# Scores ahead of the across-chunk products, and three reordered operations on VectorE, in a linear-attention and expert-routing kernel

## Chip, cores and metric

The kernel runs on one NeuronCore of one Trainium2 chip. The metric is device time in microseconds (us) of one execution. TensorE does the matrix products, VectorE (DVE in the profile) and ScalarE (ACT) read their results from PSUM, GpSimd (POOL) and SyncE (SP) do the rest and the transfers.

## The reference, cut to what matters

```python
def _linear_attention(x, Wq, Wk, Wv, Wo):
    Q = _phi((x @ Wq)...); K = _phi((x @ Wk)...); V = (x @ Wv)...
    S = jnp.cumsum(jnp.einsum('bhti,bhtj->bhtij', K, V), axis=2)
    z = jnp.cumsum(K, axis=2)
    num = jnp.einsum('bhti,bhtij->bhtj', Q, S)
    den = jnp.maximum(jnp.einsum('bhti,bhti->bht', Q, z), EPS_DEN)[..., None]
    return (num / den).transpose(0, 2, 1, 3).reshape(b, t, H * DV) @ Wo
x = x + _linear_attention(_layernorm(x, ln1_g, ln1_b), Wq, Wk, Wv, Wo)
h = _layernorm(x, ln2_g, ln2_b)
x = x + jax.nn.gelu(h @ Wf1, approximate=False) @ Wf2
```

x is 8 x 512 x 128, with 16 heads of 64; `_phi` is elu + 1. A layer norm follows, then a mixture of 8 experts (top 2 of a softmax gate, two layers of width 512), and a last layer norm.

## The kernel before

**Steps.** The attention part runs over 8 batch rows b and, in each, over 8 pairs of heads p: 64 steps, numbered g = 8b + p. The sequence of 512 is cut into four chunks of 128. Every engine has its own program, written out by hand in order, and the engines meet only through semaphores. Work of step g - 1 and g - 2 is mixed into step g, and in steps p = 2 to 7 the feed-forward part and the gate of batch row b - 1 are mixed in as well. After the 64 steps, 39 tiles of 256 routed rows go through the experts.

**TensorE in a step** issues, in this order: `columns(g-1)`, which is the state products K V of each chunk (L535, bank_u) and then the masked products inside the chunks (L542, banks_o); in p = 2 or 3 a transpose of another part; `across(g-1)`, the products of Q with the states of earlier chunks, which finish banks_o (L554); `scores(g)`, K Q inside the chunks (L563, banks_sc); `keys_t(g)`, transposes of K (L569, bank_u); the projections of Q and K for step g + 1 (L434 to L436, bank_q and bank_k); `wo_acc(g-2)` into bank_y; the projection of V (L458 to L460, into half of banks_sc); and `otr(g-1)`, the transposes of the normalised output (L446, into the other half of banks_sc).

**VectorE in a step**: `states(g-1)` sums the state products over chunks (L1296, L1298); `ot_low(g-2)` makes the low half of the transposed output from bank F, the second half of banks_sc, and from ScalarE's high half (oT_lo, L1129); then what the feed-forward part or the gate needs (`residual1`, `norm2` L1145, `norm3` L1145, `logits`, `place`); `normalise(g-1)` (L1282, L1284, L1286); `mask(g)` over both banks of scores (L1273); more of the other part (`residual2` L1191, `stats1`, `top2` L1218 to L1235, `g_high` L1187); and `q_phis`, `k_phis` of step g + 1 (L1257). In the last batch row the VectorE program also reads expert numbers into its registers (`expert(t)`, L1122) in steps p = 4 to 7, two behind each `mask`.

**ScalarE in a step**: `ktok_copy` (behind `keys_t`), the four exponential passes (L890 to L898), `v_copy`, and `ot_high(g-1)`, which makes oT_hi (L827) from the transposes. In p = 4 the four `gelus` (L856) come first; they read bank_q, bank_k and both halves of banks_sc.

Bank F is read by `ot_high` and `ot_low` and then overwritten by the scores, which is why `scores(g)` waits for `ot_lo` of g - 2. Bank E is read by `v_copy`. The state products share bank_u with the transposed keys.

Of the kernel before, what the change touches and what calls it, by code (L numbers as in the profile page):

```python
# [31 lines left out]
B, T, D = 8, 512, 128  # L32
CH = T // P
H, DH = 16, 64
PAIRS = H // 2
# [29 lines left out]
def build(nc, x_d, ln1_g, ln1_b, wq_d, wk_d, wv_d, wo_d, ln2_g, ln2_b, wf1_d, wf2_d,  # L65
# [5 lines left out]
    with ExitStack() as ctx:  # L71
# [154 lines left out]
        def ps(name, n):  # L226
# [23 lines left out]
        q_relu, q_exp, k_relu, k_exp, v_sb, kt_sb, ot_hi, yT_sb = (  # L250
            sem(n) for n in ("q_relu", "q_exp", "k_relu", "k_exp", "v_sb", "kt_sb", "ot_hi", "yT_sb"))
# [179 lines left out]
        def _(pe):  # L431
# [113 lines left out]
            def across(g):  # L545

                cur = g % 2
                pe.wait_ge(s_sb, g + 1)
                for c in range(1, CH):
                    if c == 2 and g + 1 < B * PAIRS:  # L550
                        pe.wait_ge(v_sb, min(CH + g + 1, 2 * CH * B))
                    for n, rows in enumerate(HEADS):
                        for h, hs in enumerate(HEADS):
                            mm = pe.matmul((bkG, bkH)[h][rows, blk(c, DV1)], qT[cur][hs, blk(2 * c + n, DH)],  # L554
                                           state[hs, c - 1, :], start=False, stop=(c == CH - 1))
                mm.then_inc(o_mm, 1)

            def scores(g):
                cur = g % 2
                for c in range(CH):  # L560
                    for n, rows in enumerate(HEADS):
                        for h, hs in enumerate(HEADS):
                            mm = pe.matmul((bkE, bkF)[h][rows, blk(c)], kT[cur][hs, blk(2 * c + n, DH)],  # L563
                                           qT[cur][hs, blk(c)], start=True, stop=True)
                mm.then_inc(sc_mm, 1)
# [12 lines left out]
            def step(b, p):  # L578
# [4 lines left out]
                if g > 0:  # L583
                    columns(g - 1)
                    if p == 2 and not first:
                        a_free(g - 1)
                        y_t(b - 1, bkA)
                    if p == 3 and not last:
                        b_free(g - 1)
                        front_t(b + 1)  # L590
                    across(g - 1)

                if g == 0:
                    pe.wait_ge(k_phi, 1)
                if g > 1:
                    pe.wait_ge(ot_lo, g - 1)
                if p == 4 and not first:
                    pe.wait_ge(gelu_sb, b * NF)
                scores(g)
                if p != 3:  # L600
                    keys_t(g)

# [515 lines left out]
        def _(dve):  # L1118
# [148 lines left out]
            def ot_low(g):  # L1267
                dve.wait_ge(ot_hi, g + 1)
                low(oT[1][:, :], bkF[:, :], oT[0][:, :]).then_inc(ot_lo, 1)
# [38 lines left out]
            def step(b, p):  # L1308
                g = b * PAIRS + p
                first, last = b == 0, b == B - 1  # L1310
                nxt = g + 1 < B * PAIRS
                if g > 0:
                    states(g - 1)
                if g > 1 and p != 4:
                    ot_low(g - 2)
                if not first:
                    if p == 0 and b > 1:
                        place(b - 2, bkA)
                    if p == 2:
                        residual1(b - 1, bkA)  # L1320
                    if p == 3:
                        norm2(b - 1)
                    if p == 4:
                        g_high(b - 1, (0, 1))
                    if p == 6:
                        norm3(b - 1)
                    if p == 7:
                        logits(b - 1, bkA)
                if g > 0:
                    normalise(g - 1)  # L1330
                mask(g)
                if last:
                    if p == 0:
                        plan_full_tiles()
# [539 lines left out]
```

## Time and profile before

| what | value |
|---|---|
| median of 3 runs | 725.69 us (724.81 to 725.83) |
| span of the profiled execution, first to last instruction | 696.0 us |
| its own total time | not given apart from the span; the median less the span is 29.69 us |
| TensorE matmul busy | 663.0 us, 95% |
| weight loads busy | 564.0 us, 81% |
| VectorE busy | 530.4 us, 76% |
| ScalarE busy | 426.3 us, 61% |
| GpSimd busy | 245.2 us, 35% |
| mean granted TensorE clock | 0.996 of full |

Busy times of engines overlap. The span is one execution under the profiler; the runs are timed without it. Times within the span are in us from its start.

### The profile page before, as it was taken

How to read it: one execution, taken by the hardware profiler on the slowest of the kernel's cores; microseconds unless marked ns; L12 is line 12 of the kernel's file. 1: busy time of each engine (PE TensorE's matmuls, PEld its weight loads, DVE VectorE, ACT ScalarE, POOL GpSimd, SP SyncE). 2: the span in 40 equal slices, each digit the busy share in tenths (PEclk: the TensorE clock that was granted, in tenths of full speed). 3: DMA queues.
4: the chain of work that ended last, by engine and by line, in shares of the span. 5: the costliest groups of instructions: out<-in, count | busy, mean ns of one | idle time of the engine just before them, and what ended most of it. 6: DMA issues, size and time to landing. Idle time of an engine off the chain costs nothing.

```text
span 696.0 us, 23152 instructions
## 1 busy us (share of the span) xinstructions
PE 663.0 (95%) x9314; PEld 564.0 (81%) x9314; DVE 530.4 (76%) x1565; ACT 426.3 (61%) x846; POOL 245.2 (35%) x271
## 2 busy tenths in 40 slices
PE   3899999999999999999999999999988999999995
PEld 2678888888888788888888887887778989999983
DVE  4867787887878788877878786898787777666674
ACT  4565576558466845765584668456644655666646
POOL 6200013025313512331253134123315557766664
PEclk9999999999999999999999999999999999999999
DMA  7330010001100100100011001001031224354536
GB/s 251 105 67 17 3 32 17 17 19 48 32 10 13 60 17 15 51 17 17 18 48 32 11 10 32 17 15 36 2 87 47 71 81 131 108 131 148 165 130 185
DMA packets 46521, 40.27 MB, mean 58 GB/s; under 512 B 9104, under 2 KB 41232, under 8 KB 46416
## 3 DMA queue, kind: packets, MB, share of 16 engines
q1 hardware_dynamic: 35360, 25.25, 13.1%
q0 software_dynamic: 4784, 10.39, 4.4%
q10 hardware_dynamic: 6272, 3.16, 1.5%
q8 instruction: 75, 1.23, 0.8%
q14 instruction: 30, 0.25, 0.1%
HBM read 23.12 MB, written 15.66 MB: 56 GB/s over the span
## 4 chain that ended last, share of the span: by engine, by line
PE 78%; DVE 12%; ACT 5%; issue 2%; DMA 1%; POOL 0%; DVEq 0%; ACTq 0%; POOLq 0%
PE banks_o L721 9%; PE banks_sc L563 8%; PE banks_o L542 6%; PE banks_o L554 4%; PE bank_u L535 4%; PE bank_u L569 4%; PE bank_q L434 3%; PE bank_q L436 3%; PE bank_q L435 3%; PE banks_sc L446 3%; PE bank_k L434 2%; PE bank_k L436 2%; PE bank_k L435 2%; DVE work L1257 2%; PE banks_sc L434 2%; PE bank_y L434 2%
## 5 line engine op out<-in xcount | busy, mean ns | idle before, releaser
L1723 POOL DMA_INDIRECT routed_rows<-routed,slot x64 | 63.2, 988 | 148.8 <-PE banks_sc L563 117.1
L827 ACT ACTIVATE work<-bank_u 128x384 f32<-128x384 f32 x64 | 31.5, 492 | 107.5 <-PE bank_u L569 107.5
L1273 DVE TENSOR_TENSOR work<-banks_sc,causal 128x1024 f32<-128x1024 f32 x64 | 77.9, 1218 | 0.6 <-PE banks_sc L563 0.6
L721 PE MATMUL banks_o<-w,work 128*128 x624 | 76.2, 275 | 0.0
L721 PEld LDWEIGHTS banks_o<-w,work 128*128 128x128 f32 x624 | 72.9, 192 | 0.3 <-issue 0.2
L563 PE MATMUL banks_sc<-work 64*64 64x128 f32 x2048 | 70.0, 274 | 1.1 <-ACT v_aug L827 0.7
L542 PE MATMUL banks_o<-v_aug,work 128*64 128x65 f32 x2048 | 70.6, 221 | 0.0
L1257 DVE SCALAR_TENSOR_TENSOR work<-bank_q,work 128x512 f32<-128x512 f32 x64 | 43.8, 684 | 29.4 <-ACT work L892 29.2
L1691 POOL TENSOR_SCALAR ve<-mv 128x4 f32<-128x4 f32 x24 | 4.7, 194 | 174.5 <-DVE mv L1139 174.3
L542 PEld LDWEIGHTS banks_o<-v_aug,work 128*64 128x64 f32 x2048 | 65.3, 138 | 0.0
L1257 DVE SCALAR_TENSOR_TENSOR work<-bank_k,work 128x512 f32<-128x512 f32 x64 | 44.2, 690 | 24.0 <-ACT work L898 24.0
L563 PEld LDWEIGHTS banks_sc<-work 64*64 64x64 f32 x2048 | 55.3, 133 | 8.1 <-DVE oT_lo L1129 2.7
L1713 POOL TENSOR_TENSOR gT_lo<-work,gT_hi 128x512 fp32r<-128x512 f32 x28 | 37.1, 1347 | 46.6 <-DVE gT_hi L1187 46.6
L1813 POOL DMA_INDIRECT expert_results<-work x40 | 40.1, 1004 | 21.5 <-ACT work L1023 11.3
L890 ACT ACTIVATE work<-bank_q 128x512 f32<-128x512 f32 x64 | 38.4, 600 | 14.5 <-PE bank_q L436 13.7
L1813 POOL DMA_INDIRECT expert_results<-work,xg_more x38 | 38.2, 1005 | 24.5 <-ACT work L1023 17.3
L1286 DVE TENSOR_TENSOR work<-banks_o,rden 128x512 f32<-128x512 f32 x64 | 44.3, 692 | 2.2
L1129 DVE TENSOR_TENSOR oT_lo<-banks_sc,oT_hi 128x512 fp32r<-128x512 f32 x64 | 43.6, 681 | 0.2 <-ACT oT_hi L827 0.2
L892 ACT ACTIVATE work<-work 128x512 f32<-128x512 f32 x64 | 40.5, 632 | 2.0
L898 ACT ACTIVATE work<-work 128x512 f32<-128x512 f32 x64 | 40.4, 632 | 2.0
L554 PE MATMUL banks_o<-state,work 64*64 64x65 f32 x1536 | 37.1, 226 | 4.0 <-DVE state L1298 3.8
L446 PEld LDWEIGHTS banks_sc<-ident,work 128*128 128x128 f32 x256 | 31.8, 141 | 10.4 <-DVE work L1286 1.1
(324 smaller groups left out, 1796.2 us busy)
## 6 DMA issues: line engine op xcount, KB each, us to landing
work<-in_L_attn_x SPq DMA_DIRECT2D x16, 256.0 KB, 3.4
work<-routed_rows SPq DMA_DIRECT2D x20, 132.0 KB, 2.3
xg_more<-routed_rows SPq DMA_DIRECT2D x19, 132.0 KB, 2.1
stage<-in_L_ffn_w SPq DMA_DIRECT2D x8, 256.0 KB, 2.6
moe_input<-routed SPq DMA_DIRECT2D x8, 256.0 KB, 2.6
work<-moe_input ACTq DMA_DIRECT2D x8, 256.0 KB
v_aug<-expert_results SPq DMA_DIRECT2D x4, 512.0 KB, 6.1
out<-work SPq DMA_DIRECT2D x6, 256.0 KB, 2.9
```

Of the source, the lines that this page charges most:

```text
L434: pe.matmul(out, w[0][:, wcols], m[0][:, mcols], start=first, stop=False)
L446: mm = pe.transpose(out[:, blk(c)], src(c), ident[:, :])
L542: pe.matmul((bkG, bkH)[h][rows, blk(c, DV1)], am[h][:, c, rows], va[:, c, 2 * p + h, :], start=(c == 0), stop=False)
L554: mm = pe.matmul((bkG, bkH)[h][rows, blk(c, DV1)], qT[cur][hs, blk(2 * c + n, DH)], state[hs, c - 1, :], start=False, stop=(c == CH - 1))
L563: mm = pe.matmul((bkE, bkF)[h][rows, blk(c)], kT[cur][hs, blk(2 * c + n, DH)], qT[cur][hs, blk(c)], start=True, stop=True)
L721: mm = pe.matmul(Y[t % 2][:, blk(k)], hTe[t % 2][:, f, blk(k)], w2[:, bass.ds(e[t] * F + f * D, D)], start=(f == 0), stop=(f == NF - 1))
L1129: return dve.tensor_tensor(out, whole, f32(high), ALU.subtract)
L1257: return dve.scalar_tensor_tensor(out=out, in0=pre[:, :], scalar=0.0, in1=e, op0=ALU.max, op1=ALU.add)
L1273: dve.tensor_tensor(am_all, sc_banks.rearrange("p (x s) -> p x s", s=P), causal[:, :].unsqueeze(1).broadcast_to([P, 2 * CH, P]), ALU.mult) ...
L1286: dve.tensor_tensor(on.rearrange("p c (h j) -> p h c j", h=2), o4[:, :, :, 0:DH], rden[:, :].rearrange("p (h c) -> p h c", h=2).unsqueeze( ...
L1723: pool.indirect_dma_start(rows_d, bass.IndirectOffsetOnAxis(slot[:, k, c:c + 1], 0), routed[:, c, k, :], None).then_inc(sct, 16)
L1813: pool.indirect_dma_start(res_d, bass.IndirectOffsetOnAxis(xg[n][:, k, D:D + 1].bitcast(U32), 0), yw[t % YRING][:, k, :], None).then_inc(r ...
```

## The change

On TensorE `scores(g)` now stands ahead of `across(g-1)`. The wait for `v_sb` that stood inside `across` stands ahead of the scores, with a wait for `k_phi` of the step. On VectorE `ot_low(g-2)` stands ahead of `states(g-1)`, and `mask(g)` ahead of `normalise(g-1)`. No instruction that computes is added or removed.

```diff
@@ across
                 for c in range(1, CH):
-                    if c == 2 and g + 1 < B * PAIRS:
-                        pe.wait_ge(v_sb, min(CH + g + 1, 2 * CH * B))
                     for n, rows in enumerate(HEADS):
@@ TensorE step
                         b_free(g - 1)
                         front_t(b + 1)
-                    across(g - 1)
-
-                if g == 0:
-                    pe.wait_ge(k_phi, 1)
+
+                pe.wait_ge(k_phi, g + 1)
+                if g > 0:
+                    pe.wait_ge(v_sb, min(CH + g, 2 * CH * B))
                 if g > 1:
                     pe.wait_ge(ot_lo, g - 1)
                 if p == 4 and not first:
                     pe.wait_ge(gelu_sb, b * NF)
                 scores(g)
+                if g > 0:
+                    across(g - 1)
                 if p != 3:
                     keys_t(g)
@@ VectorE step
+                if g > 1 and p != 4:
+                    ot_low(g - 2)
                 if g > 0:
                     states(g - 1)
-                if g > 1 and p != 4:
-                    ot_low(g - 2)
@@
+                mask(g)
                 if g > 0:
                     normalise(g - 1)
-                mask(g)
```

VectorE in one step p = 2 before: L1296 and L1298 are the state sums, L1129 the low half, L1169 the first residual, L1282 to L1286 the normalising, L1273 the mask, L1134 the statistics.

```order
L1257 SCALAR_TENSOR_TENSOR work<-bank_k,work 128x512
L1296 COPY state<-bank_u 128x65
L1298 TENSOR_TENSOR state<-bank_u,state 128x65 x2
L1129 TENSOR_TENSOR oT_lo<-banks_sc,oT_hi 128x512
L1169 TENSOR_TENSOR work<-bank_q,work 128x512
L1282 TENSOR_SCALAR den<-banks_o 128x8
L1284 RECIPROCAL rden<-den 128x8
L1286 TENSOR_TENSOR work<-banks_o,rden 128x2x4x64
L1273 TENSOR_TENSOR work<-banks_sc,causal 128x1024
L1134 BN_STATS stats<-work 128x6 x4
```

The same place of the same engine in the changed kernel:

```order
L1257 SCALAR_TENSOR_TENSOR work<-bank_k,work 128x512
L1129 TENSOR_TENSOR oT_lo<-banks_sc,oT_hi 128x512
L1296 COPY state<-bank_u 128x65
L1298 TENSOR_TENSOR state<-bank_u,state 128x65 x2
L1169 TENSOR_TENSOR work<-bank_q,work 128x512
L1273 TENSOR_TENSOR work<-banks_sc,causal 128x1024
L1282 TENSOR_SCALAR den<-banks_o 128x8
L1284 RECIPROCAL rden<-den 128x8
L1286 TENSOR_TENSOR work<-banks_o,rden 128x2x4x64
L1134 BN_STATS stats<-work 128x6 x4
```

The low half moved up past two lines, and the mask past three; what follows the pair of mask and normalising (here the statistics) follows the normalising now and followed the mask before.

TensorE at the start of one step p = 3 in the changed kernel, with its waits (L561 is the scores there and L552 the across-chunk products; bank_k<- is `front_t`, bank_u<-ident the transpose `h2_t` of the feed-forward part):

```order
L542 MATMUL banks_o<-v_aug,work 64x65 x15
L446 MATMUL bank_k<-ident,work 128x128 [waits ln_x0,k_phi]
L446 MATMUL bank_k<-ident,work 128x128 x3
L561 MATMUL banks_sc<-work 64x128 [waits ot_lo,v_sb,k_phi]
L561 MATMUL banks_sc<-work 64x128 x15
L552 MATMUL banks_o<-state,work 64x65 [waits s_sb]
L552 MATMUL banks_o<-state,work 64x65 x11
L446 MATMUL bank_u<-ident,work 128x128 [waits ln_x1]
```

The wait for `ot_lo` now stands ahead of both groups, and the across-chunk products run behind the scores.

## Rows read from the trace of the kernel before

**Rows 1.** The page, part 1: busy us, share of the span, instructions

```profile
PE 663.0 (95%) x9314; PEld 564.0 (81%) x9314; DVE 530.4 (76%) x1565; ACT 426.3 (61%) x846; POOL 245.2 (35%) x271
```

**Rows 2.** Waits: of line L554 (us, times), and of the list of waits

```profile
  DVE state L1298: 11.4, 30
...
PEld banks_sc L563 <- DVE oT_lo L1129: 2.7, 17, 0.2
```

**Rows 3.** Timeline of a step p = 1: start us, us, engine, line

```profile
272.25 0.57 PE L535 MATMUL bank_u<-v_aug,work 128*64 128x65 f32 x12
...
272.61 0.59 ACT L827 ACTIVATE oT_hi<-banks_sc 128x512 fp32r<-128x512 f32 x1
...
273.53 0.68 DVE L1129 TENSOR_TENSOR oT_lo<-banks_sc,oT_hi 128x512 fp32r<-128x512 f32 x1
...
273.68 0.58 PE L554 MATMUL banks_o<-state,work 64*64 64x65 f32 x24
...
274.26 1.10 PE L563 MATMUL banks_sc<-work 64*64 64x128 f32 x32
...
275.30 0.55 PE L569 MATMUL bank_u<-ident,work 128*128 128x128 f32 x3
```

**Rows 4.** Timeline from a step p = 2 (begins at 279.00) into p = 3 (286.46)

```profile
281.71 1.10 PE L563 MATMUL banks_sc<-work 64*64 64x128 f32 x32
...
284.34 0.86 DVE L1134 BATCH_NORM_STATS2 stats<-work 128x6 f32<-128x128 f32 x4
...
287.23 1.27 POOL L1701 TENSOR_TENSOR work<-work 128x512 f32<-128x512 f32 x1
...
288.53 1.21 DVE L1145 TENSOR_SCALAR work<-work,mv,rstd 128x128 f32<-128x128 f32 x4
...
289.86 0.66 PE L446 MATMUL bank_u<-ident,work 128*128 128x128 f32 x4
```

**Rows 5.** Timeline of a step p = 4: last gelus, across, scores, keys

```profile
297.82 1.10 ACT L856 ACTIVATE work<-banks_sc 128x512 f32<-128x512 f32 x2
...
298.69 0.58 PE L554 MATMUL banks_o<-state,work 64*64 64x65 f32 x24
...
299.09 1.08 PE L563 MATMUL banks_sc<-work 64*64 64x128 f32 x32
...
300.10 0.55 PE L569 MATMUL bank_u<-ident,work 128*128 128x128 f32 x3
```

**Rows 6.** Timeline of the step p = 5 that begins at 306.60

```profile
304.19 0.59 ACT L827 ACTIVATE oT_hi<-banks_sc 128x512 fp32r<-128x512 f32 x1
...
310.93 0.68 DVE L1191 TENSOR_TENSOR work<-bank_k,work 128x512 f32<-128x512 f32 x1
...
311.87 0.39 PE L434 MATMUL bank_k<-hT_hi,wk_hi 128*128 128x512 f32 x1
```

**Rows 7.** Timeline of the step p = 7 that begins at 322.01

```profile
324.44 0.16 DVE L1282 TENSOR_SCALAR den<-banks_o 128x8 f32<-128x8 f32 x1
...
325.48 1.21 DVE L1273 TENSOR_TENSOR work<-banks_sc,causal 128x1024 f32<-128x1024 f32 x1
...
326.61 0.36 DVE L1218 MAX8 top<-gate_exp 128x8 f32<-128x8 f32 x4
...
328.40 0.68 DVE L1257 SCALAR_TENSOR_TENSOR work<-bank_q,work 128x512 f32<-128x512 f32 x1
...
329.14 0.19 PE L517 MATMUL bank_q<-chosen,before 128*128 128x32 bf16 x1 [0.30 <-DVE work L1257]
```

**Rows 8.** Line L1122 (ns min/median/max), and the last batch row's step p = 4

```profile
L1122 DVEq TENSOR_LOAD <-tile_e x39: 298/305/572, 492.2 to 663.1; - x39
L1122 DVEq FUSED_REGOPS  x39: 183/190/216, 492.8 to 663.5; - x39
...
493.78 0.76 DVE L1187 CAST gT_hi<-work 128x512 fp32r<-128x512 f32 x2 [0.18 <-issue]
...
495.39 0.51 PE L434 MATMUL bank_q<-gT_hi,wf_hi 128*128 128x512 f32 x1 [0.25 <-DVE work L1257]
```

## Prediction

> **What bounds the kernel now.** I read the busy times first. TensorE's matmuls are busy 95% of the span, VectorE 76%, ScalarE 61% [rows 1], so the time is TensorE's plus what it waits for. The waits come next: on VectorE's state sums it waits 11.4 us in 30 places, and on the low half 2.7 us in 17 [rows 2]. These are what the change can reach. The rest is read from the timeline of single steps, because the question is which wait ends last at one point: the start of the transposes of K behind scores and across-chunk products. I call it the keys point; TensorE's work behind it is not reordered.
>
> A plain step p = 1 [rows 3]: state products start at 272.25, across at 273.68 (1.43 later), scores at 274.26, keys point 275.30. So the scores group takes 1.04 from start to start. Unhindered, across takes 0.40 (298.69 to 299.09) [rows 5]; in p = 1 it takes 0.58, because the scores wait for the low half, which ends at 274.21 [rows 3].
>
> **The change, part by part.** Nothing is added but waits, so the sum is made of shifts. Across has to be done before the keys point in either order. The rule for a step is: keys point moves by (new start of scores less old start) + 0.40. The change pays only where the scores start more than 0.40 earlier.
>
> *Low half ahead of the state sums (all steps but p = 4).* In p = 1 the high half is copied until 273.20 and the low half starts at 273.53 [rows 3]. Ahead of the sums it starts at 273.23 at best, 0.30 earlier, so the scores start 0.30 earlier and the keys point comes **0.10 later** (I take 0.11). ScalarE's chain of exponentials, V copy and high half hangs from the preceding keys point, so a later one brings no relief. Steps p = 2 and 6 repeat this (high half late, low half directly behind the sums): 0.12 each. In p = 5, 7 and 0 the high half is done before the low half could start (304.78 for the step that begins at 306.60 [rows 6]); the scores start right behind the masked products, at 1.43, and the wait of 0.19 goes: **0.19 earlier** to begin with.
>
> *p = 3.* The second norm starts at 288.53, 0.03 behind GpSimd's sum (287.23 + 1.27), and the transposes that read it start at 289.86, where TensorE would be anyway [rows 4]. GpSimd's sum hangs on statistics that start at 284.34, behind mask and normalising of p = 2. Now the mask starts only after the scores: 281.71 less 0.29, plus 1.10 and 0.06 of signal, is 282.58; the mask holds VectorE 1.13 (325.48 to 326.61) and normalising 1.04 (324.44 to 325.48) [rows 7], so the statistics start at 284.75, 0.41 later. The step itself starts 0.12 later; the remaining 0.3 meets TensorE at the transposes, with 0.06 of signal behind the norm: **+0.26**.
>
> *p = 4.* Scores also wait for the gelus, which end at 298.92, 0.23 behind 298.69 [rows 5]. Across covered that; now scores start at 298.98, only 0.11 earlier than 299.09: **+0.29**.
>
> *p = 5.* TensorE gains 0.19, but scores end 306.60 + 1.43 + 1.10 = 309.13, the mask starts at 309.19, and 1.13 + 1.04 later, at 311.36, VectorE begins the second residual (310.93 before). Its 0.68 end at 312.04 and the K projection that overwrites its input starts at 312.10 instead of 311.87 [rows 6]: **+0.23**. Before, normalising ran during the scores; now VectorE idles there. That is what is queued behind the moved mask.
>
> *p = 7.* Likewise: mask at 324.60, both done at 326.77 instead of 326.61. Top-2 and the Q operation behind it gate the rank products (329.14, with an idle before it) [rows 7]: **+0.16**.
>
> *p = 0.* Nothing waits for VectorE at the end: **-0.19**.
>
> Sum of a batch row: -0.19 + 0.11 + 0.12 + 0.26 + 0.29 + 0.23 + 0.12 + 0.16 = +1.10. There are six such stretches, from p = 1 of b = 1 to p = 0 of b = 7: **+6.6**. In b = 0, with p = 0 of b = 1, there is no feed-forward part; the first step gains an estimated 0.5 of its long wait on the state sums (part of the 11.4 of [rows 2]), the others lose 0.1 each: **0**.
>
> *Last batch row.* There two expert numbers are read into VectorE's registers behind the mask in p = 4 to 7. A read is 0.305 + 0.190 us [rows 8], two are 1.0, with gaps I take 1.2. They lie beside the mask's 1.21 now. Behind normalising they stand behind 1.13 of mask and 0.44 of its first two operations, and nothing covers them but its last 0.69. From the mask's start to what follows this is 1.13 + 0.44 + 1.2 = 2.8 instead of 1.4, while the mask starts 0.4 earlier: what follows is 0.9 to 1.0 later. In p = 4 this is the gelu copies (493.78) and then Q, for which the second feed-forward product waits already (495.39, idle 0.25 before it) [rows 8]: +0.76. In p = 5 it is the residual, as above: +0.88. In p = 6 four planning operations: +0.3. In p = 7 and the handover to the experts top-2 and the last low half: +0.76. With 0.11, 0.12 and 0.33 for p = 1 to 3 (planning operations on VectorE add 0.07 in p = 3): **+3.3**.
>
> The experts' part has TensorE at its own pace, and nothing in it moves; I carry the delay through.
>
> Total: 6.6 + 0 + 3.3 = +9.9. The span would be 705.9. Durations are those of the profiled execution; 725.69 - 696.0 = 29.69 us lie around its span and stay, so the time is 725.69 + 9.9 = **735.6 us**.
>
> One term rests on when the register reads begin. The trace's direct evidence is that VectorE stands idle 0.18 on "issue" just ahead of 493.78 [rows 8]: the reads were still running when the mask was done. The Trainium skill, Perfetto Trace Analysis, section Sequencer Loop, says that engine instructions are pushed into a queue while control instructions run in the sequencer. By that rule the reads could run ahead of the queued mask and normalising, and cost nothing.
>
> **The rivals.** *A, faster:* the moved low half frees the scores by 0.40 or more in nearly all steps, and nothing behind mask or normalising is late. Then each of 56 steps gains 0.19, and the state waits go: about 11.3 us of the 14.1 in [rows 2], so 714.4. For it: half of the steps have the high half early. Against it: 273.20 in [rows 3] is ScalarE's, and it is 0.95 behind the step's start. The point of decision is whether the low half ends 0.40 earlier than now.
>
> *B, no change:* TensorE is bound by its own work at 95%, gains and losses of a few tenths cancel: 725.7. For it: the waits are 2% of the span. Against: the terms have one sign in six of eight steps. The Trainium skill, Perfetto Trace Analysis, section Identifying the Most-Contended Engine, holds matmul busy time to be a poor measure and asks for the weight loads' busy share, here 81%.
>
> *C, register reads run ahead:* the last row costs about 0.6 for p = 4 to 7 and 0.56 for the rest, 1.2 instead of 3.3: 733.5.
>
> *D, slower, but p = 3 and p = 5 hidden:* if those late values are not the last to come, a batch row costs 1.10 - 0.26 - 0.42 = 0.4, and all 2.5 + 3.3: 731.5.
>
> **How the numbers follow.** Forecast (a batch row costs 0.9 to 1.3, the last one near 3; its own range 733.5 to 738) 0.50; C 0.16; D 0.14; more than 740, by delays that add up in the last row and the handover, 0.07; A or part of it 0.08; B 0.05. The range leaves out A, B and the far end: 730.5 to 740. About 0.2% (1.5 us) is what a measurement of this kernel can tell from no change: slower by more than that 0.87, within it 0.05, faster 0.08.
>
> **What would show it.** In the trace after: a batch row of 65.0 instead of 63.9 us; scores in p = 1 starting 1.7 behind the state products with TensorE idle on the low half; the K projection of p = 5 waiting for line L1191, the transposes of p = 3 for L1145, the scores of p = 4 for a gelu; VectorE idle during the scores; in the last batch row "issue" idle ahead of the gelu copies near 1 us. Wrong would be: a batch row at or under 63.9, or the scores of p = 1 starting 1.43 behind the state products, which would mean that the high half comes earlier than I have it.

## The result, and where the time went

The changed kernel takes 753.32 us (751.62 to 756.89, 4 runs), the kernel before 725.58 us (724.81 to 725.83, 4 runs): a ratio of 1.0392, with a 95% interval of 1.0364 to 1.042. That is 27.7 us slower; forecast were 9.9.

The same program takes 696.5 to 697.1 us (medians) on some chips and 724.0 to 726.0 on others; the mean granted clock of two profiles of the kernel before is 0.996 and 0.984. I call them the 697 chips (there were three) and the 725 chips (three, and the one of this result, which may be one of the three). Each chip was met in one session only, so that the difference belongs to the chip, and not to the time or the place of a session, is not shown; "chip" stands for both below. The trace of before that stands ahead of the prediction has a span of 696.0 us, which is that of a 697 chip, while the times beside it are those of a 725 chip. The prediction took the difference, 29.69 us, for time around the span; in every run below the time is 1.7 us over the span.

Page, part 1, of the changed kernel, to set beside [rows 1]:

```profile
PE 665.2 (88%) x9314; PEld 571.0 (76%) x9314; DVE 534.2 (71%) x1565; ACT 426.2 (57%) x846; POOL 247.1 (33%) x271
```

The work is the same; what grew is waiting. Two lines of its list of waits (engine, line, releaser: us, times, longest), where PEld is TensorE's weight loads and "issue" stands for no releaser that the profile shows, and below them the releasers of line L552 (the across-chunk products):

```profile
PEld banks_sc L561 <- issue: 23.9, 39, 1.6
...
PE banks_sc L561 <- DVE oT_lo L1129: 17.6, 27, 1.4
```

```profile
  issue: 6.4, 14
  DVE state L1298: 0.4, 1
```

The wait for the state sums went (11.4 us in [rows 2], 0.4 now); a wait for the low half took its place (2.7 in [rows 2], 17.6 now). Grown are the waits of across for nothing that the profile shows: 6.4 us in 14 places, where the kernel before had 1.2 in 7.

The step p = 1 that answers to [rows 3], timeline of the changed kernel:

```profile
283.86 0.57 PE L535 MATMUL bank_u<-v_aug,work 128*64 128x65 f32 x12
...
284.85 0.69 DVE L1129 TENSOR_TENSOR oT_lo<-banks_sc,oT_hi 128x512 fp32r<-128x512 f32 x1 [0.28 <-ACT oT_hi L827]
...
285.69 1.10 PE L561 MATMUL banks_sc<-work 64*64 64x128 f32 x32 [0.33 <-DVE oT_lo L1129]
...
286.59 0.56 PE L552 MATMUL banks_o<-state,work 64*64 64x65 f32 x24
...
287.07 0.55 PE L567 MATMUL bank_u<-ident,work 128*128 128x128 f32 x3
287.10 0.96 POOL L1723 DMA_INDIRECT routed_rows<-routed,slot  x1 [4.14 <-PE banks_sc L561]
...
288.48 0.49 ACT L827 ACTIVATE work<-bank_u 128x384 f32<-128x384 f32 x1 [3.66 <-PE bank_u L567]
```

The order part is as forecast: scores 1.83 behind the state products (1.7 forecast), idle on the low half. The last row was not forecast: ScalarE reads the transposed keys at 288.48, while the record of those transposes ends at 287.07 + 0.55 = 287.62. The signal (TensorE's increment of the semaphore that ScalarE waits for) came 0.86 late, and GpSimd had begun an indirect scatter of routed rows at 287.10.

Two steps on, in p = 3 (answers to [rows 4]), the same timeline:

```profile
301.29 1.10 PE L561 MATMUL banks_sc<-work 64*64 64x128 f32 x32
...
301.85 1.05 POOL L1723 DMA_INDIRECT routed_rows<-routed,slot  x1 [0.17 <-issue]
...
302.22 0.52 PE L552 MATMUL banks_o<-state,work 64*64 64x65 f32 x19
...
303.16 0.34 PE L552 MATMUL banks_o<-state,work 64*64 64x65 f32 x4 [0.42 <-issue]
303.21 0.98 POOL L1723 DMA_INDIRECT routed_rows<-routed,slot  x1 [0.30 <-issue]
303.90 0.21 PE L552 MATMUL banks_o<-state,work 64*64 64x65 f32 x1 [0.40 <-issue]
304.04 0.66 PE L446 MATMUL bank_u<-ident,work 128*128 128x128 f32 x4
...
304.70 1.23 DVE L1273 TENSOR_TENSOR work<-banks_sc,causal 128x1024 f32<-128x1024 f32 x1 [1.77 <-remote]
...
306.37 0.78 ACT L847 ACTIVATE work<-bank_u,cols 128x512 f32<-128x512 f32 x1 [3.53 <-remote]
```

The scatter begins at 301.85; the across group then runs 19 products, pauses, 4, pauses, 1. It takes 1.82 from its start to the next instruction instead of 0.45 to 0.5. The mask behind the scores starts at 304.70, although the scores' record ends at 301.29 + 1.10 = 302.39. The mask waits for these scores, 2.3 us longer than their record. The step is 13.85 us long. In the kernel before, p = 3 on the 697 chips takes 10.80.

### The profile page after: what moved, and what is told of

It reads as the page before. It is cut to its first block, busy times and chain, and to the rows that moved or that the text cites. A ratio compares the mean times of both kernels' runs of the same rounds, so it can differ in the third digit from the quotient of the medians.

```text
span 752.8 us, 23215 instructions
## 1 busy us (share of the span) xinstructions
PE 665.2 (88%) x9314; PEld 571.0 (76%) x9314; DVE 534.2 (71%) x1565; ACT 426.2 (57%) x846; POOL 247.1 (33%) x271
## 4 chain that ended last, share of the span: by engine, by line
PE 55%; ACT 21%; DVE 13%; another core or an unknown queue 5%; issue 4%; DMA 1%; DVEq 1%; POOL 0%; ACTq 0%; POOLq 0%
PE banks_sc L561 8%; PE banks_o L721 8%; PE banks_o L542 3%; DVE work L1273 3%; ACT work L898 3%; PE bank_q L436 3%; DVE oT_lo L1129 3%; PE bank_u L567 3%; ACT work L896 2%; PE bank_q L434 2%; ACT v_aug L827 2%; ACT oT_hi L827 2%; PE bank_q L435 2%; ACT work L892 2%
## 5 line engine op out<-in xcount | busy, mean ns | idle before, releaser
L1273 DVE TENSOR_TENSOR work<-banks_sc,causal 128x1024 f32<-128x1024 f32 x64 | 78.4, 1224 | 37.3 <-PE banks_sc L561 28.0
L561 PE MATMUL banks_sc<-work 64*64 64x128 f32 x2048 | 70.7, 275 | 20.5 <-DVE oT_lo L1129 17.6
L561 PEld LDWEIGHTS banks_sc<-work 64*64 64x64 f32 x2048 | 56.1, 132 | 28.1 <-issue 23.9
L721 PEld LDWEIGHTS banks_o<-w,work 128*128 128x128 f32 x624 | 74.7, 195 | 0.4 <-issue 0.2
L542 PE MATMUL banks_o<-v_aug,work 128*64 128x65 f32 x2048 | 70.6, 221 | 0.0
L542 PEld LDWEIGHTS banks_o<-v_aug,work 128*64 128x64 f32 x2048 | 65.3, 138 | 0.0
L1813 POOL DMA_INDIRECT expert_results<-work x40 | 40.7, 1018 | 38.2 <-ACT work L1023 22.2
L1129 DVE TENSOR_TENSOR oT_lo<-banks_sc,oT_hi 128x512 fp32r<-128x512 f32 x64 | 43.9, 686 | 10.8 <-ACT oT_hi L827 10.8
L1813 POOL DMA_INDIRECT expert_results<-work,xg_more x38 | 38.7, 1020 | 27.7 <-issue 18.1
L890 ACT ACTIVATE work<-bank_q 128x512 f32<-128x512 f32 x64 | 38.3, 599 | 14.4 <-PE bank_q L436 13.7
L1286 DVE TENSOR_TENSOR work<-banks_o,rden 128x512 f32<-128x512 f32 x64 | 44.2, 691 | 2.2
L1519 DVE TENSOR_SCALAR work<-banks_sc,b_cols 128x256 f32<-128x256 f32 x78 | 34.2, 478 | 14.7 <-remote 7.4
L896 ACT ACTIVATE work<-bank_k 128x512 f32<-128x512 f32 x64 | 37.4, 585 | 6.0 <-PE bank_k L436 5.7
```

Of the source, the lines that this page charges most:

```text
L542: pe.matmul((bkG, bkH)[h][rows, blk(c, DV1)], am[h][:, c, rows], va[:, c, 2 * p + h, :], start=(c == 0), stop=False)
L721: mm = pe.matmul(Y[t % 2][:, blk(k)], hTe[t % 2][:, f, blk(k)], w2[:, bass.ds(e[t] * F + f * D, D)], start=(f == 0), stop=(f == NF - 1))
L896: act.activation(e_k, bkB[:, :], ACT.Relu, scale=-1.0).then_inc(k_relu, 1)
L1129: return dve.tensor_tensor(out, whole, f32(high), ALU.subtract)
L1273: dve.tensor_tensor(am_all, sc_banks.rearrange("p (x s) -> p x s", s=P), causal[:, :].unsqueeze(1).broadcast_to([P, 2 * CH, P]), ALU.mult) ...
L1813: pool.indirect_dma_start(res_d, bass.IndirectOffsetOnAxis(xg[n][:, k, D:D + 1].bitcast(U32), 0), yw[t % YRING][:, k, :], None).then_inc(r ...
```

## Experiments

Step lengths below are from one start of L535 to the next, in a batch row from b = 2 on. A ratio is to the kernel before on the same chip.

### 1. Each half of the change alone, a shift, a later scatter (697 chip, before 696.54)

e1, TensorE's new order with VectorE's old one (from the changed kernel):

```diff
-                if g > 1 and p != 4:
-                    ot_low(g - 2)
                 if g > 0:
                     states(g - 1)
+                if g > 1 and p != 4:
+                    ot_low(g - 2)
...
-                mask(g)
                 if g > 0:
                     normalise(g - 1)
+                mask(g)
```

> The kernel before with TensorE's part of the change alone (scores ahead of across, with its waits); VectorE keeps its order. Order theory (a step costs what its last wait costs): the scores still wait for the low half behind the state sums, so in a plain step they start 2.02 us behind the state products as before and across comes on top: +0.40 us in most steps, about 3 us a batch row, 20 to 28 us in all. Stall theory (the unpredicted part of the changed kernel, about 4 us in p = 2 and 3 of each batch row from b = 2 on, belongs to TensorE's new order): the late semaphores behind the across-chunk products of p = 1 and p = 3 stand here too, on top. If the stall belongs to VectorE's order, none is seen.

Measured: 738.46, ratio 1.0593 (1.0575 to 1.0611). Steps p = 0 to 7 are 7.26, 7.39, 7.78, 11.4, 9.88, 8.57, 8.69, 8.61: every one is longer. The scores wait for a low half that stands behind the state sums (34.0 us in 53 places), as I expected, and across comes on top. What I had not counted is the way back: VectorE's normalising, still ahead of the mask, now waits for across (70.4 us in 58 places), and the mask and all behind it are late with it. So the cost is 41.9 us and not 20 to 28. VectorE's part of the change takes most of it back.

e2, the old TensorE order and the old low half, with the mask ahead of normalising (from the kernel before):

```diff
+                mask(g)
                 if g > 0:
                     normalise(g - 1)
-                mask(g)
```

> The kernel before with the mask ahead of normalising on VectorE alone; TensorE keeps its order. Order theory: normalising begins 2.3 us later than it could, everything behind the pair is late by about 0.9 us: p = 5 +0.9 (K projection waits for the second residual), p = 7 about +0.8, p = 3 about +0.8 (second norm late through the statistics), so 2.5 us a batch row and 15 to 22 us in all. Stall theory: no late semaphores of TensorE, since its order is that of before; p = 2 near 7.5 us and p = 3 under 12.

Measured: 718.74, ratio 1.0317 (1.03 to 1.0335). p = 5 +0.94, p = 7 +0.77, p = 3 +0.66: where a value that VectorE makes behind normalising gates TensorE. The whole, 22.2 us, is at the upper end of the 15 to 22 expected.

e3, 64 more TensorE instructions ahead of the loop, so that its instruction fetches fall elsewhere:

```diff
+            for _ in range(32):
+                pe.transpose(bkY[:, 0:P], ident[:, :], ident[:, :])
```

> The changed kernel with 32 transposes of the identity into an unused bank at the start of TensorE's program: 64 more TensorE instructions (weight loads and matmuls), which moves every 16 KB instruction fetch of TensorE to a place 64 instructions earlier in its stream and changes nothing else. Fetch theory (TensorE stalls where the fetch of its next instructions falls on the scores and across groups of p = 1 and p = 3): the stalls there vanish or move, and the time changes by several us, 725 + 10 to 745. Scatter theory (GpSimd's indirect transfers running during these groups stall TensorE): p = 2 and p = 3 stay at 8.5 and 13.8 us, time 752 to 757.

Measured: 710.43, ratio 1.0191 (1.0174 to 1.0208).

e4, GpSimd's scatters wait for the next Q projection instead of the scores, 1.1 us later in p = 0 and 2.2 to 2.7 later in p = 1 and p = 3:

```diff
-                        pool.wait_ge(sc_mm, b * PAIRS + c + 1)
+                        pool.wait_ge(q_mm, b * PAIRS + (0, 1, 3, 3)[c] + 2)
```

> The changed kernel with GpSimd's scatters released by the Q projection of their step in place of its scores, and the last two by that of p = 3, so that none overlaps scores or across. Scatter theory: the late semaphores vanish, p = 2 comes to 7.6 and p = 3 to 11.1 us, a batch row to 65 us, and the time to about 736 (less than 740). Fetch theory: p = 2 and p = 3 stay within 0.3 us of 8.5 and 13.8, the time within 3 us of 753.

Measured: 707.75, ratio 1.0164 (1.014 to 1.0188). Neither stalls here, but e5 shows that the changed kernel doesn't either on such a chip; none of the four runs tells anything of the late signals.

### 2. Both kernels again, and two versions (697 chip, before 697.05)

e5 is the changed kernel without an edit, e6 the kernel before.

> The changed kernel, unedited, again. The two runs that were to move or empty the stall of p = 2 and p = 3 both lost it, and so did the two that hold one part of the change each; the kernel before took 696.5 us beside them and 725.6 beside the changed kernel. Order theory with the stall tied to the place of the run: beside a kernel before of about 697 us this takes 706 to 710 us, p = 2 takes 7.6 and p = 3 11.1 us, and no semaphore of TensorE is late; beside one of about 725 us the stall is back. Fetch theory and scatter theory (the stall belongs to this very instruction stream): p = 2 and p = 3 take 8.5 and 13.8 us again, and the time is 20 to 30 us over the kernel before in either case.

> The kernel before, unedited, as a run of its own, so that its profile, span and time come from one execution. Expected: the time is the span and 1.7 us, as in the changed kernel's run, so that the 725.6 us beside the first result were a span of about 724 and not one of 696 with 30 us around it. If the time is 725 and the span 696, the rest lies outside the span.

Measured: e5 710.37, ratio 1.0182 (1.0165 to 1.0199); e6 696.88, 0.9991 (0.998 to 1.0001). Here the change costs 13.3 us, not 27.7. Timeline of e5: a step p = 1, the p = 3 and p = 5 behind it, and the last row's p = 4:

```profile
277.55 0.69 DVE L1129 TENSOR_TENSOR oT_lo<-banks_sc,oT_hi 128x512 fp32r<-128x512 f32 x1 [0.28 <-ACT oT_hi L827]
...
278.39 1.10 PE L561 MATMUL banks_sc<-work 64*64 64x128 f32 x32 [0.32 <-DVE oT_lo L1129]
...
279.77 0.55 PE L567 MATMUL bank_u<-ident,work 128*128 128x128 f32 x3
...
280.36 0.49 ACT L827 ACTIVATE work<-bank_u 128x384 f32<-128x384 f32 x1 [2.84 <-PE bank_u L567]
...
294.80 0.66 PE L446 MATMUL bank_u<-ident,work 128*128 128x128 f32 x4 [0.23 <-DVE work L1145]
...
303.99 1.10 PE L561 MATMUL banks_sc<-work 64*64 64x128 f32 x32 [0.31 <-ACT work L856]
...
317.39 0.50 PE L434 MATMUL bank_k<-hT_hi,wk_hi 128*128 128x512 f32 x1 [0.32 <-DVE work L1191]
...
504.40 0.76 DVE L1187 CAST gT_hi<-work 128x512 fp32r<-128x512 f32 x2 [0.87 <-issue]
```

Each wait that the prediction named is there. Between the keys transposes (279.77 + 0.55) and ScalarE's copy lie 0.04 us, where the result's trace of the same kernel had 0.86.

e7, the new order in two steps of a batch row only, with the second residual ahead of normalising in p = 5:

```diff
+        def ahead(g):
+            return (g % PAIRS == 0 and g // PAIRS > 1) or (g % PAIRS == 5 and 0 < g // PAIRS < B - 1)
...
+                    if not ahead(g):
+                        across(g - 1)
...
                 if ahead(g):
                     mask(g)
+                    if p == 5 and not last:
+                        residual2(b - 1, bkB)
```

> The kernel before with the changed order only in the steps where the low half can come early: p = 0 from b = 2 on and p = 5 of b = 1 to 6; there VectorE does the second residual between mask and normalising in p = 5. All other steps as before. Order theory: each such step gains 0.19 us, 12 of them 2.3 us, 0.3% faster than the kernel before. Against it: if the mask ahead of normalising makes something later after all, p = 5 takes 7.2 us or more and p = 0 6.75 or more, and the time is unchanged or slower.

Measured: 693.59, ratio 0.9958 (0.9947 to 0.997). p = 0 6.52 instead of 6.75, p = 5 6.97 instead of 7.21, p = 6 8.32 instead of 8.24: 0.4% faster than the kernel before, a small gain, but with the whole interval under 1.

e8, the changed kernel with the second residual ahead of normalising:

```diff
+                if p == 5 and not first and not last:
+                    residual2(b - 1, bkB)
```

> The changed kernel with the second residual of p = 5 (b = 1 to 6) between mask and normalising. Order theory: the K projection no longer waits for it, p = 5 takes 7.0 to 7.1 instead of 7.55 us, and the time is 2.5 to 3 us under that of the changed kernel on the same chip. If the K projection was held by something else, p = 5 stays at 7.5.

Measured: 706.37, ratio 1.0138 (1.0116 to 1.016), p = 5 6.97 instead of 7.56. So that step's delay is the residual behind mask and normalising.

### 3. The same on a 725 chip (before 724.80)

e9 is the changed kernel, e11 the kernel before, e10 is e3.

> The changed kernel, unedited, on another chip. If the stall comes with the chip or session (the kernel before near 725 us beside it), it is back here: p = 3 near 13.8 us and 20 us or more in all. If the kernel before is near 697 us, this takes 708 to 711, the third reading of the clean cost (1.8 to 2.0% over the kernel before).

> The kernel before, unedited, with a profile from the same chip as the changed kernel's. Where it takes 725 us, its own trace shows where the 28 us lie: late semaphores of TensorE in the experts' part (most of the first result's second half of excess) or also in steps p = 1 and 3. Where it takes 697 us, no semaphore is late by more than 0.3 us in the attention part.

> The changed kernel with TensorE's instruction fetches moved by 64 instructions, again. Where the kernel before takes 725 us and the changed one stalls: by the fetch theory p = 3 takes 11.1 us here, by the scatter theory 13.8. Where nothing stalls it takes 709 to 711 us, as in its first run, and tells nothing.

Measured: e9 751.28, ratio 1.0357 (1.0318 to 1.0397); e11 725.88, 1.0007 (0.9991 to 1.0023); e10 753.77, 1.0392 (1.0352 to 1.0432), with p = 2 at 8.2 and p = 3 at 13.7 as in e9. The fetches ran at most 0.7 us earlier in p = 3 than in e9, though, and still beside scores and across, so that e10 alone clears them only in part. Two later traces do the rest: in e12 the scores of a step p = 5 take 3.9 us (183.0 to 186.9) while the instruction queue moves nothing from 182.0 to 187.6, and in e18 a fetch at 294.33 falls on across in p = 3 and nothing stalls. e9 to e11 is 25.4 us, e5 to e6 13.5: the chip makes the other half.

The kernel before is stalled as well, in p = 3 alone. Timeline of e11:

```profile
291.72 1.05 POOL L1723 DMA_INDIRECT routed_rows<-routed,slot  x1 [0.17 <-issue]
291.93 1.50 PE L563 MATMUL banks_sc<-work 64*64 64x128 f32 x29
...
293.69 0.45 PE L563 MATMUL banks_sc<-work 64*64 64x128 f32 x3 [0.27 <-issue]
```

Its scores are stretched beside a scatter. Its across group had all but run before that (its record ends at 292.11, 0.39 behind the scatter's start, and its signal comes 1.6 late), and p = 3 is 11.98 instead of 10.80.

### 4. What runs beside those products (725 chip, before 726.04)

Besides the instruction fetches, what moves data in p = 1 and p = 3 is GpSimd's scatters and, in p = 3, two loads of x by SyncE. e12 moves the scatters, e13 the loads, e14 both; e15 is e7.

```diff
-                        pool.wait_ge(sc_mm, b * PAIRS + c + 1)
-                        scatter_chunk(b - 2, c)
-                paced(0)
-                paced(1)
+                chunks((0, 1))
...
                     g_low(b - 1, range(NF))
+                    chunks((2, 3))
```

```diff
                     sp.wait_ge(xx_sb, b)
+                    sp.wait_ge(sc_mm, b * PAIRS + 5)
                     sp.dma_start(xres, x_of(b)).then_inc(ld_xres, 16)
```

> The changed kernel with GpSimd's eight scatters of routed rows of a batch row moved: the first four back to back in p = 0 (done 7.6 us after its start, ahead of the across-chunk products of p = 1), the last four behind the last low halves of the gelus, at the end of p = 4. None of them then runs beside the scores and across-chunk products of p = 1 and p = 3. Where the kernel before takes 725 us (step lengths of the changed kernel there 8.2 in p = 2 and 13.7 in p = 3): theory S, the scatters beside the 64x64 products hold TensorE's signals back: p = 2 at 7.6 and p = 3 at 11.0 to 11.5, total near 736. Theory L, the two loads of x do it: 8.2 to 7.6 in p = 2 (the loads are not there) remains unexplained, 13.7 in p = 3, total 748 to 753. Theory N, neither transfer has to do with it: 8.2 and 13.7, 751. Where the kernel before takes 697, all theories: 709 to 711.

> The changed kernel with the two 256 KB loads of x (lines 335 and 341) moved from the middle of p = 3 to behind the scores of p = 4. Where the kernel before takes 725: theory S: 8.2 in p = 2 and 13.7 in p = 3 as before the move, total 751. Theory L: p = 3 at 11 to 12, p = 2 unchanged at 8.2, total 738 to 742. Theory N: no difference, 751. Where the kernel before takes 697, all theories: 709 to 711.

> Both moves together: nothing but instruction fetches and the experts' weight runs beside the scores and across-chunk products of p = 1 and p = 3. Where the kernel before takes 725: theory S 736 and theory L 736 (a transfer of either kind suffices: both moves are needed, each alone does little); theory N 751. Where the kernel before takes 697: 709 to 711.

> The kernel before with the changed order in p = 0 and p = 5 alone and the second residual ahead of normalising in p = 5, again. Where the kernel before takes 697: 693 to 694. Where it takes 725: its p = 3 has the old order, so the late signals should cost it what they cost the kernel before; by the order alone 722 to 723. If late signals come in p = 0 or p = 5 too, 725 or more.

Measured: e12 753.27, ratio 1.0374 (1.0351 to 1.0397); e13 753.96, 1.0399 (1.0348 to 1.045); e14 752.51, 1.0374 (1.0349 to 1.04); e15 723.88, 0.9966 (0.9952 to 0.9981).

By their totals all of e12 to e14 say "neither transfer", and that reading would be wrong. e13 leaves the steps at 8.2 to 8.5 and 13.7 to 14.4. e12 and e14 have p = 2 at 7.6 and p = 3 at 11.0 to 11.3, as on a 697 chip, but p = 1 at 7.5 to 7.7 instead of 6.9 and p = 5 at 10.1 to 11.3 instead of 7.6. Timeline of e12, p = 5:

```profile
319.23 0.97 POOL L1723 DMA_INDIRECT routed_rows<-routed,slot  x1 [0.30 <-issue]
...
320.27 0.69 PE L561 MATMUL banks_sc<-work 64*64 64x128 f32 x8
320.51 0.96 POOL L1723 DMA_INDIRECT routed_rows<-routed,slot  x1 [0.30 <-issue]
...
321.27 0.45 PE L561 MATMUL banks_sc<-work 64*64 64x128 f32 x5 [0.31 <-issue]
321.77 0.95 POOL L1723 DMA_INDIRECT routed_rows<-routed,slot  x1 [0.30 <-issue]
...
322.00 0.46 PE L561 MATMUL banks_sc<-work 64*64 64x128 f32 x5 [0.28 <-issue]
322.75 0.45 PE L561 MATMUL banks_sc<-work 64*64 64x128 f32 x4 [0.29 <-issue]
```

The stall went with the scatters, and onto the scores. In p = 1 one scatter now falls beside the state products and the masked products, which are 128 x 64, and those signals are late too (0.3 to 1.1 us): the state products are held back, not 64x64 products alone. The scores of p = 5 now run in bursts of 4 or 5 products every 0.74 us, where 32 usually take 1.1.

### 5. Scatters where there are no 64x64 products

```diff
-                        pool.wait_ge(sc_mm, b * PAIRS + c + 1)
+                        if c < 2:
+                            pool.wait_ge(kt_mm, b * PAIRS + c + 1)
+                        else:
+                            pool.wait_ge(h2_mm, b)
```

e16 is the changed kernel with this, e17 is e7 with it. They met a 697 chip (before 696.50), and e18 is e16 again on a 725 chip (before 724.01). The scatters now run beside projections and transposes, products of 128 rows by 128 or 512.

> The changed kernel with the scatters of a batch row at places where TensorE has no 64x64 products: the first two behind the keys transposes of p = 0, the next two behind those of p = 1 (10.3 us after the start of p = 0, done at 12.7, the next state products at 13.5), the last four behind the across-chunk products of p = 3 (25 to 30, the next state products at 32.2). Where the kernel before takes 725 us: theory S (a scatter that runs beside 64x64 products holds TensorE; the stall went with the scatters from p = 3 to p = 5 in e12): p = 1 at 6.9, p = 2 at 7.6, p = 3 at 11.0 to 11.3 and p = 5 at 7.6, some 3 us less in each of six rows, total 735 to 740. Rival: scatters hold TensorE wherever they run: the stall turns up beside them in p = 2 or in the rest of p = 3, 750. Where the kernel before takes 697: 709 to 711 by both, and it tells nothing.

> The kernel before with the changed order in p = 0 and p = 5 alone (e7), and the scatters placed as in e16. Where the kernel before takes 725: by theory S its p = 3 falls from 12.0 to 10.8, 7 us in six rows, on top of the 2 us of e7: 716 to 718. By the rival 723 to 724 as e15. Where the kernel before takes 697: 693 to 694 by both.

> The kernel of e16 again, for a chip on which the kernel before takes 725 us. There theory S: p = 2 at 7.6, p = 3 at 11.0 to 11.3, p = 5 at 7.6, total 735 to 740; rival, scatters hold TensorE wherever they run: 750, with the stall in p = 2 or in the rest of p = 3. Where the kernel before takes 697: 708 by both.

Measured: e16 708.09, ratio 1.0167 (1.015 to 1.0185); e17 695.34, 0.9967 (0.9951 to 0.9983); e18 729.58, ratio 1.0071 (1.0052 to 1.0091), 22 us less than e9's 751.28 and 24 less than the result, and under the 735 to 740 expected. Beside the kernel before on the same chip e18 costs 5.6 us, e9 26.5. Timeline of e18, p = 3:

```profile
293.02 1.10 PE L561 MATMUL banks_sc<-work 64*64 64x128 f32 x32
...
293.94 0.53 PE L552 MATMUL banks_o<-state,work 64*64 64x65 f32 x24
...
295.29 0.78 ACT L847 ACTIVATE work<-bank_u,cols 128x512 f32<-128x512 f32 x1 [0.72 <-PE bank_u L446]
...
295.53 1.05 POOL L1723 DMA_INDIRECT routed_rows<-routed,slot  x1 [2.15 <-PE bank_u L446]
```

No pause, and every step of e18 is within 0.05 us of e16's on a 697 chip. The two loads of x still run beside scores and across (from 293.41 on), and do no harm. Whether scatters beside the large products hold signals as well is not shown: some increments there leave no record of their own, but no step is longer than in e16. That scatters beside the small products cost the other half on a 725 chip is thereby shown: with the scatters moved, and nothing else, it is gone.

## Where the 27.7 us are

The masked products (L542) run in the attention part alone, so the start of the last one splits the span. Line L542 in e6, e11, e5, e9, e18 (ns min/median/max, first and last start), one fence each:

```profile
L542 PE MATMUL banks_o<-v_aug,work x2048: 219/222/223, 24.4 to 520.8; 128*64 128x65 f32 x187
```

```profile
L542 PE MATMUL banks_o<-v_aug,work x2048: 219/222/223, 24.7 to 528.1; 128*64 128x65 f32 x187
```

```profile
L542 PE MATMUL banks_o<-v_aug,work x2048: 219/222/223, 24.0 to 532.4; 128*64 128x65 f32 x187
```

```profile
L542 PE MATMUL banks_o<-v_aug,work x2048: 219/222/224, 23.5 to 552.8; 128*64 128x65 f32 x187
```

```profile
L542 PE MATMUL banks_o<-v_aug,work x2048: 219/222/223, 24.1 to 532.2; 128*64 128x65 f32 x187
```

| kernel | attention part, 697 chip | 725 chip | rest of the span, 697 | 725 |
|---|---|---|---|---|
| before (e6, e11) | 520.8 | 528.1 | 174.9 | 196.8 |
| changed (e5, e9) | 532.4 | 552.8 | 177.0 | 197.0 |
| changed, scatters between (e16, e18) | 531.4 | 532.2 | 174.3 | 193.4 |

The first L542 starts at 23.5 to 24.7 in these five, so that the differences are good to about 1 us.

On a 725 chip the changed kernel loses 552.8 - 528.1 = 24.7 us in the attention part and nothing behind it. Of these, 532.4 - 520.8 = 11.6 are the order of the steps, which costs the same on every chip. The other 13.1 are (552.8 - 532.4) - (528.1 - 520.8) = 20.4 - 7.3: what the late signals cost the changed kernel less what they cost the kernel before. The result's own trace has the last L542 at 556.0, 3.2 more, most of it in the same two steps (8.2 to 8.5 and 13.8 to 14.4, and 15.5 in the last batch row). Together 27.9 between the profiled runs, for 27.7 between the medians.

**The rest of the span follows the granted clock.** Views by window of the part behind the last L542 in e6, e5 and e16, all on 697 chips; the third number from the end is the granted clock:

```profile
520.80:695.70 174.90, 163.77 (x1326) 152.79 (x1320) 116.68 (x384) 107.34 (x279) 107.63 (x110) 0.98 0.40 120
```

```profile
532.40:709.40 177.00, 165.86 (x1324) 154.68 (x1318) 117.46 (x389) 107.22 (x279) 106.97 (x110) 0.97 0.39 118
```

```profile
531.40:705.70 174.30, 162.47 (x1326) 151.53 (x1320) 117.37 (x389) 107.01 (x279) 107.19 (x110) 0.99 0.40 120
```

TensorE's busy time differs by what the length differs (165.86 and 163.77; 177.0 and 174.9). The changed kernel in e4 and e8, at 0.99, has 174.0 and 173.9, less than the kernel before in e6. So no cost of the change shows in the experts' part; the 2.1 us of e5 over e6 go with a longer time at the lower of TensorE's two clocks (1.2 instead of 2.4 GHz).

## Why the prediction was wrong, by its steps

**The step that failed** is "Durations are those of the profiled execution; 725.69 - 696.0 = 29.69 us lie around its span and stay". They lay inside the span of a chip on which TensorE is held up; the profile shown was of a chip without that. All six groups of rows from single steps were those of an undisturbed TensorE, and the sum made from them is the cost on such a chip. It was carried to a chip where the change has a second cost. The sign was right, and 17.8 us of size were missing: 753.32, where the range ended at 740.

**The unpriced mechanism.** The prediction's "TensorE's work behind it is not reordered" was true, but GpSimd's scatters stand beside it. They are released by the scores (or, in p = 3, by the sum L1701 ahead of them). With across behind the scores, a second 64x64 group, and with it the keys transposes, lies inside the scatters' time. The mask and normalising wait for the held signals, and ScalarE for the transposed keys: p = 2 +0.6 and p = 3 +2.6 (e9 against e5), against +1.2 in p = 3 of the kernel before (e11 against e6).

**The sum, on the chip for which it was made** (lengths in us, e6 and e5):

| step | before | changed | measured | forecast |
|---|---|---|---|---|
| p = 0 | 6.75 | 6.53 | -0.22 | -0.19 |
| p = 1 | 6.75 | 6.92 | +0.17 | +0.11 |
| p = 2 | 7.46 | 7.62 | +0.16 | +0.12 |
| p = 3 | 10.80 | 11.11 | +0.31 | +0.26 |
| p = 4 | 9.33 | 9.67 | +0.34 | +0.29 |
| p = 5 | 7.20 | 7.56 | +0.36 | +0.23 |
| p = 6 | 8.24 | 8.40 | +0.16 | +0.12 |
| p = 7 | 7.41 | 7.60 | +0.19 | +0.16 |
| batch row | 63.94 | 65.41 | +1.47 | +1.10 |

All eight signs hold. **"Keys point moves by (new start of scores less old start) + 0.40"**: the low half starts 0.29 earlier as forecast (0.99 behind the state products, 1.28 in [rows 3]) and ends at 278.24, but the scores start at 278.39, 0.15 behind it; in [rows 3] the distance is 0.05. The group then takes 1.38 to the keys point where the old one took 1.04, so the constant is 0.34. Net +0.16 for p = 1 instead of +0.10, and a like 0.05 in the steps that the low half gates.

**p = 3, p = 4, p = 5, p = 7**: the waits for L1145, a gelu and L1191 are there (0.23, 0.31 and 0.32 in the rows of e5), and so is that for the Q operation (5.7 us in 6 places in e5, 3.2 before). p = 5 was mis-sized by 0.13. Its K projection starts 5.52 behind the step's start, as forecast (5.50), but its first product takes 0.50 after the wait, where the row before shows 0.39 [rows 6]; the sum has no term for that. e8 confirms the cause of the delay: with the residual ahead of normalising the step takes 6.97.

**p = 0, and b = 0**: p = 0 is -0.22. p = 1 of b = 0 gains 0.65 (6.94 to 6.29), p = 3 and p = 4 stay, and the other four, with p = 0 of b = 1, lose about 0.16 each; the sum is +0.1 to +0.2, near the 0 forecast.

**Last batch row, +3.3**: measured p = 3 +0.37, p = 4 +1.22, p = 5 +0.97, p = 6 +0.22, p = 7 +0.25 (forecast 0.33, 0.76, 0.88, 0.3, and 0.76 with the handover); with 0.30 for p = 1 and 2 some 3.3. p = 4 was 0.46 under, p = 7 some 0.5 over: that the sum of the row agrees is in part luck. The register reads cost about what was said: "issue" idle ahead of the gelu copies is 0.87 (near 1 forecast, 0.18 in [rows 8]), and the first read starts at 502.8, with the last operation of normalising (502.83). So rival C fell. By its rule (the Trainium skill, Perfetto Trace Analysis, section Sequencer Loop) the reads could have run ahead of the queued mask; by the trace they don't.

**Total of the order part**: 11.6 us in the attention part against 9.9, and 13.3 in the whole time beside the same kernel before. The 2.1 left over in the two profiles stand in the experts' part, where nothing moves, as forecast; they go with the granted clock, as shown above.

**Rivals.** A fell: the low half ends 0.29 earlier, not 0.40. (Its 11.3 us are not the 56 x 0.19 = 10.6 beside them.) B fell; the terms have one sign in seven of eight steps, not in six. D fell: neither p = 3 nor p = 5 is hidden. "More than 740" came true, but by another cause than the delays that it names. Missing among them was a transfer on another queue that the moved products would meet.

## What to carry to other kernels

- Before a time is added to a span, ask whether span and times are of the same chip: 29.7 us "around the span" should have been a question, since every run here has 1.7. A cost that the shown trace cannot hold then belongs in the range.
- Small products (64x64 and 128 x 64 here) can be held back by what other engines issue beside them, as they were by scatters on the 725 chips. When a group is moved, list what GpSimd issues in its new place; and look at step lengths, not totals: e12 to e14 had one total and two opposite meanings.
- Reordering TensorE pays only where its new first group has all inputs. Two of eight steps had (e7, e15), 0.4% on a 697 chip and 0.3% on a 725 chip; the other six cost more than these gave.
- Compare the granted clock before a difference of 2 or 3 us is put to the change.

## What the runs showed of the hardware

- **Late signals.** I set each record of a semaphore increment by TensorE beside the recorded end of the last product that raises that semaphore. In the attention part over 0.25 us late are 61 of 654 in the result, 52 of 654 in e9, 13 of 629 in e11, and none in e5, e6 and e18; the median is 0.015. Between product and signal a scatter was running in 58 of the 61. They are up to 2.3 us late, and up to 4.9 in the last batch row. The Trainium skill, Perfetto Trace Analysis, section Summary: the profiler window per engine type, says that TensorE's end is an estimate and that the signal is not in it; the trace agrees, and shows how large the gap can be. So whether the signal was late or the product itself, these records do not tell.
- **Missing records.** On 725 chips some increments leave no record of their own: 34 of 656 in the attention part of e18, and 80 of 258 in the experts' part of the result, against 0 and 2 in e5. Such a place must not be read as a late signal.
- **Bursts.** In e12 the pauses are visible in the records themselves: 4 or 5 products of 64x64, then 0.28 to 0.31 us of nothing, until 0.77 us behind the end of the last scatter (322.72, and 323.49 for the first burst of 9). That TensorE's own records pause speaks for products held back, and not for signals alone.
- **The clock fell during pauses of TensorE.** In e11, in the experts' part, TensorE idled 3.22 us and came back at the lower clock, which had set in 0.9 us before its return. In the result's last batch row it is 2.78 us of idle time (to 515.79) and the lower clock from 516.3, part of the 15.5 above. The experts' part has a mean granted clock of 0.941 in e11 and 0.985 in e6, which is 11.6 and 2.6 us of full-speed time less; so at most 9 of the 22 us between them are the clock. Line of e11, in which the product takes 0.79 where 0.48 is usual at full clock:

```profile
555.66 0.79 PE L434 MATMUL banks_sc<-h2T_hi,wf_hi 128*128 128x512 f32 x1 [3.22 <-ACT work L856]
```

- **What is open.** Why one chip does this and another doesn't is not shown; 725 and 697 chips have the same step lengths to 0.05 us once the scatters are out of the way, so they compute alike there. The other 22 us between them in the kernel before lie in the experts' part (174.9 and 196.8), where GpSimd issues 78 more scatters (L1813) and increments are late too (34 of 188 in e11, none of 255 in e6); I expect the same cause for what is not the clock, and for the pauses at which it falls, and no run tested it. Nor was e17, 0.3% faster than the kernel before on a 697 chip, run on a 725 chip, where it should also save the 7.3 us that the kernel before loses there.
- The Trainium skill, DMA: Bandwidth & Descriptors, section Latency and other measured facts, names contention at the ports of GpSimd's descriptor rings as its best guess, not certain, for two of the DMA engines being slower than the others. Whether TensorE's products or signals meet that too, no run here shows.
